# Rounding x_t by a casting DMA from GpSimd instead of by ScalarE, in a gated cross-attention and FFN block

## The reference

```
x   : (4, 512, 512)   ctx : (4, 512, 256)
q   = ctx @ Wq.T + bq ;  k = ctx @ Wk.T + bk             # 128 wide
att = softmax(q @ k.T, axis=-1)                           # (512, 512) a batch
y   = layernorm(x) @ att.T                                # einsum('bln,bmn->blm')
x1  = x + tanh(g_xattn) * y
z   = layernorm(x1) * ln_weight + ln_bias
out = x1 + tanh(g_ffn) * ((z @ sign(W).T) * max|W| * gamma + beta)
```

## Time and profile before

| | us |
|---|---|
| median of 3 runs | 123.74 (123.06 to 123.81) |
| the profiled execution | 123.59 |
| its span (first to last instruction) | 121.8 |
| PE busy | 116.7 (96%) |
| POOL busy | 94.7 (78%) |
| DVE busy | 94.2 (77%) |
| ACT busy | 86.5 (71%) |
| HBM read | 12.59 MB |

### The profile page before, as it was taken

One profiled execution on the slowest core, in us unless ns is written; L12 is line 12 of the kernel. 1 busy time (PEld: TensorE's weight loads), 2 busy tenths in 40 slices (PEclk: granted clock), 3 DMA queues, 4 the chain that ended last, 5 costly groups with the idle time before them and its releaser, 6 DMA issues.

```text
span 121.8 us, 1883 instructions
## 1 busy us (share of the span) xinstructions
PE 116.7 (96%) x565; PEld 94.7 (78%) x565; DVE 94.2 (77%) x186; ACT 86.5 (71%) x184; POOL 94.7 (78%) x108
## 2 busy tenths in 40 slices
PE   7799999999999999999999999999999999999980
PEld 6477887888887877878889888888888888888870
DVE  0159499999888996769966993799849948988991
ACT  3365999999997988476998795659987972245200
POOL 2046995869077998999995999994748999999970
PEclk9999999999999999999999999999999999999999
DMA  3999499833454400027871402457000012220045
GB/s 104 243 378 384 154 405 351 330 112 132 95 192 147 141 31 5 3 86 252 264 258 16 156 5 86 158 181 240 24 3 0 3 63 115 86 86 0 0 154 190
DMA packets 10394, 17.15 MB, mean 141 GB/s; under 512 B 1809, under 2 KB 2321, under 8 KB 10385
## 3 DMA queue, kind: packets, MB, share of 16 engines
q1 hardware_dynamic: 9808, 16.78, 39.9%
q10 hardware_dynamic: 576, 0.26, 0.8%
HBM read 12.59 MB, written 4.19 MB: 138 GB/s over the span
## 4 chain that ended last, share of the span: by engine, by line
PE 92%; DMA 4%; DVE 2%; issue 0%; SPq 0%
PE ps_y L420 37%; PE ps_ffn L433 23%; PE ps_score L355 7%; PE ps_turn L387 6%; DMA ctx_sb<-in_ctx_t_dram 4%; PE ps_score L387 3%; PE ps_y L387 3%; PE ps_ffn L325 2%; PE ps_turn L325 2%; PE ps_y L378 2%; PE ps_turn L355 1%; PE ps_score L364 1%; PE ps_ffn L334 1%; PE ps_y L497 1%; PE ps_ffn L449 1%; PE ps_y L343 1%
## 5 line engine op out<-in xcount | busy, mean ns | idle before, releaser
L915 POOL TENSOR_TENSOR xt_lo<-xt_raw,xt_hi 128x512 fp32r<-128x512 f32 x16 | 21.1, 1319 | 3.9 <-ACT xt_hi L561 2.9
L420 PE MATMUL ps_y<-pt_hi,xt_hi 128*128 128x512 f32 x64 | 18.1, 404 | 0.2 <-issue 0.2
L420 PE MATMUL ps_y<-pt_hi,xt_lo 128*128 128x512 f32 x64 | 17.5, 395 | 0.0
L420 PE MATMUL ps_y<-pt_lo,xt_hi 128*128 128x512 f32 x64 | 17.5, 395 | 0.0
L433 PE MATMUL ps_ffn<-w_sign,zt_hi 128*128 128x512 f32 x60 | 17.2, 408 | 0.0
L433 PE MATMUL ps_ffn<-w_sign,zt_lo 128*128 128x512 f32 x60 | 16.5, 396 | 0.0
L549 ACT ACTIVATE prob<-ps_score,neg_max 128x512 f32<-128x512 f32 x14 | 9.5, 681 | 9.7 <-DVE neg_max L698 9.6
L420 PEld LDWEIGHTS ps_y<-pt_hi,xt_lo 128*128 128x128 f32 x64 | 12.0, 188 | 2.9
L420 PEld LDWEIGHTS ps_y<-pt_lo,xt_hi 128*128 128x128 f32 x64 | 12.0, 188 | 2.9
L420 PEld LDWEIGHTS ps_y<-pt_hi,xt_hi 128*128 128x128 f32 x64 | 11.5, 188 | 2.6 <-issue 0.4
L433 PEld LDWEIGHTS ps_ffn<-w_sign,zt_lo 128*128 128x128 f32 x60 | 11.3, 188 | 2.8
(11 more groups left out here) (184 smaller groups left out, 270.2 us busy)
## 6 DMA issues: line engine op xcount, KB each, us to landing
xt_raw<-in_x_t_dram SPq DMA_DIRECT2D x16, 256.0 KB, 2.9
ctx_sb<-in_ctx_t_dram SPq DMA_DIRECT2D x8, 256.0 KB, 5.2
x_sb<-in_x_dram SPq DMA_DIRECT2D x8, 256.0 KB, 4.4
ctx_sb<-in_x_dram SPq DMA_DIRECT2D x8, 256.0 KB, 5.6
out_dram<-x SPq DMA_DIRECT2D x8, 256.0 KB, 2.0
out_dram<-ctx_sb SPq DMA_DIRECT2D x7, 256.0 KB, 2.1
w_raw<-in_weight_t_dram SPq DMA_DIRECT2D x4, 256.0 KB, 7.0
ln_w<-in_ln_weight_dram SPq DMA_DIRECT2D x1, 256.0 KB, 6.3
```

The source lines that it names most:

```text
L420: mm = pe.matmul(ps_y[t % 2][:, :], lhs[:, t, k, :], rhs[:, k, :], start=(k == 0 and i == 0), stop=(k == KN - 1 and i == 2))
L915: nc.gpsimd.tensor_tensor(xt_lo[:, t, :, :], xt_raw[:, t, :, :], xt_hi[:, t, :, :].bitcast(f32), ALU.subtract).then_inc(xt_lo_done, 1)
```

## The change

In batches 1 to 3, `xt_hi` is no longer written by ACT from `xt_raw`. POOL issues a DMA that reads `x_t` again from HBM and converts float32 to f32r on its way into `xt_hi`. The raw copy is still loaded by SP, and POOL still subtracts. The four DMAs of a `back(b)` stand at four places of POOL's list, and each waits for the same `y_ready` count as the activation did. `attend` and POOL's subtraction wait for a semaphore of the DMA's own.

```
         def attend(b, t):
...
-                pe.wait_ge(xt_hi_done, T * b + t + 1)
+                pe.wait_ge(*((xt_cast[t], 16 * b) if b else (xt_hi_done, t + 1)))
...
         # ScalarE
             def split_xt(b, t):
-                act.wait_ge(xt_in[t], 16 * (b + 1))
-                act.wait_ge(y_ready, T * (b - 1) + t + 1)
-                nc.scalar.activation(xt_hi[:, t, :, :], xt_raw[:, t, :, :], ACT.Copy)\
-                         .then_inc(xt_hi_done, 1)
+                pass
...
         # GpSimd
+            def cast_xt(b, t):
+                pool.wait_ge(y_ready, T * (b - 1) + t + 1)
+                nc.gpsimd.dma_start(xt_hi[:, t, :, :], x_t[b, t, :, :, :]).then_inc(xt_cast[t], 16)
+
             def split_xt(b, t):
-                pool.wait_ge(xt_hi_done, T * b + t + 1)
+                if b > 0:
+                    pool.wait_ge(xt_cast[t], 16 * b)
+                    pool.wait_ge(xt_in[t], 16 * (b + 1))
+                else:
+                    pool.wait_ge(xt_hi_done, T * b + t + 1)
...
             def back(b):
+                cast_xt(b + 1, 0)
                 add_shift(b, 0)
+                cast_xt(b + 1, 1)
                 add_shift(b, 1)
                 if b > 0:
                     power2(b, 0)
...
                 add_shift(b, 2)
                 power2(b, 1)
                 split_xt(b + 1, 1)
+                cast_xt(b + 1, 2)
                 add_ffn(b, 0)
+                cast_xt(b + 1, 3)
                 add_shift(b, 3)
                 add_ffn(b, 1)
                 split_xt(b + 1, 2)
```

More of the change, by code:

```diff
@@ L134, in flamingo_block_kernel @@
         xt_in = [sem(f"xt_in{t}") for t in range(T)]
+        xt_cast = [sem(f"xt_cast{t}") for t in range(T)]
         out_stored = [[sem(f"out_stored{i}_{t}") for t in range(T)] for i in range(2)]
```

## The result

The changed kernel takes 143.26 us (median, 142.59 to 145.07), the kernel before 123.72: a ratio of 1.158 (95% interval 1.154 to 1.163), 15.8% slower. One of its four executions, 145.07 us, had a lower granted clock than the others (0.93 against 0.94 to 0.95); the median of the other three is 142.83. 129.2 was predicted, with a range from 125.2 to 134.0. The sign was right, and 14 us are unaccounted for.

A forecast was written before the change was run, and what follows sets the result against it. PE, busy 96% of the span, was taken as the bound. PE's delay of 5.4 us plus 0.1 us for the last stores made 5.5 us, giving 129.1 from the profiled 123.59; 129.2 us was predicted, range 125.2 to 134.0.

The forecast's parts named there:

- the term for ACT: Twelve activations, 7.4 us, leave ACT; PE never waits for ACT, so worth 0.0, at most 0.2 us.
- The price c: Time that one DMA issue holds POOL: taken as 1.0 us, with 0, 0.44 and 1.3 kept as range.
- Rival 1: The issue on POOL is as cheap as SP's, 0.44 us: 1.7 us of waiting, 125.4 us; chance 0.20.
- The prediction's second estimate: From the Trainium skill's page, 0.4 us on top of SP's 0.44: an issue of 0.84 us, 127.3 us in all.
- Rival 2: The issue runs beside POOL's arithmetic, at most a few hundredths of a us: no change, 123.7 us; chance 0.10.
- Step 1: In back(0), four issues ahead of the third subtraction with 0.06 us slack: PE waits 3.9 us.
- Steps 2 and 3: POOL's gaps close in back(1), no new wait, and in back(2), where PE's total delay becomes 5.4 us.
- the end: POOL's last addition comes 5.8 us later, at 123.2; its store costs 0.1 us beyond PE's 5.4.
- Landing: The first DMA of back(0) lands at 44.1 us, 0.7 us before POOL's subtraction; other transfers have more operations between.
- What it adds: Twelve DMA issues in POOL's list, four per back; the bytes cost nothing by themselves, the y_ready waits hold nothing up.
- the signs of being wrong: Profile signs: gap at 56 us not four issues or before the first pass, POOL's gaps staying, PE waiting for zw or scores.

The follow-up runs named there:

- e13: Kernel before without the twelve roundings of batches 1 to 3, by ACT or DMA; xt_hi keeps batch 0's values: 123.62 us, ratio 0.998.
- e8: Changed kernel with the third and fourth DMA of each back moved up, ahead of scale_x: 126.25 us, ratio 1.019.
- e1: Changed kernel with POOL's own rounding of xt_raw in place of each of the twelve DMAs: 128.38 us, ratio 1.039.
- e10: Changed kernel with two DMAs of two tiles (512 KB) per back in place of four of one tile: 127.08 us, ratio 1.028.
- e6: Kernel before plus twelve POOL copies on all 128 partitions at the places of the DMAs: 127.80 us, ratio 1.031.
- e5: Kernel before plus twelve POOL copies on 32 partitions at the places of the DMAs: 142.17 us, ratio 1.144.
- e4: Changed kernel with tile 0's centring in batches 1 to 3 reading PSUM in place of one SBUF operand: 131.71 us, ratio 1.064.
- e2: Changed kernel with one more POOL wait per back, behind the fourth DMA, for its own preceding addition: 127.63 us, ratio 1.033.
- e9: Changed kernel with ACT rounding tiles 2 and 3 again, DMAs kept for tiles 0 and 1: 125.26 us, ratio 1.014.
- e12: Kernel before plus twelve POOL copies on 32 partitions, each followed by a POOL wait for it to end: 129.47 us, ratio 1.049.
- e7: Kernel before plus twelve POOL DMAs of 8 KB, 64 bytes to each of 128 partitions: 142.19 us, ratio 1.148.
- e3: Kernel before plus twelve POOL DMAs of the same size without conversion, into w_raw's memory: 142.41 us, ratio 1.151.

## Why the prediction was wrong

The kernel before had this view of all its centrings (ns min/median/max):

```profile
L739 DVE SCALAR_TENSOR_TENSOR zw<-x,neg_mean,ln_w x8: 732/1031/1786, 26.6 to 93.4; 128x512 f32<-128x512 f32 x8
L739 DVE SCALAR_TENSOR_TENSOR zw<-ctx_sb,neg_mean,ln_w x8: 732/1495/1895, 52.3 to 111.4; 128x512 f32<-128x512 f32 x8
```

- **What bounds the kernel, and the term for ACT**: right. 0.0 to 0.2 us was said, e13 measured 0.2 us (0.2%) with an interval that ends at no change.
- **The price c**: 1.0 taken, 0.58 measured; it was mis-sized by 0.42. Rival 1's row, SP's issue at 0.44, was nearer than POOL's power at 1.02. By the prediction's own formula, 4c - 0.06, the measured c gives 2.3 us and 126.0, so this term misses by 3 us in the other direction. The prediction's second estimate, 0.84, was too high as well. Rival 2, an issue beside POOL's arithmetic, is out: each issue shows on POOL for 0.57 us or more, and the third subtraction came 2.3 us later (58.21 in place of 55.90).
- **Step 1 (four issues, no slack)**: the mechanism is right where it is alone: e8 grew by 2.3 us of span, e1 waits 2.5 us for the third `xt_lo` with c = 0.61. In the changed kernel the third subtraction ended at 58.21, inside the hole, where PE stood still for `zw` already; the 0.4 us that PE waited for `xt_lo` are those for the second one. So the sign of this kernel's change came out as forecast, but its size has another cause.
- **Steps 2 and 3, the end**: at c = 0.58 the sum has POOL absorbed in `back(1)` and `back(2)`. In the changed kernel it even idled 10.8 us for ACT's squares, late in turn for DVE.
- **Landing**: right, 2.9 us, no slower by the conversion; POOL waited for it only in e10.
- **What failed** is the step "What it adds". It names what stands behind a late DMA "on POOL", subtractions, `scale_x` and `power2`, and takes an issue for a duration in POOL's list, whatever it is made of. It never asks who shares with POOL. With it fails the sentence of step 1 that what stands behind on DVE can be no later than 2c: the centring took 8.76 us, and so ended some 8 us later than at its usual length. DVE's centring was in none of the rivals; a wait of PE for `zw` was only among the signs of being wrong, without a price. The rows were there: the centring took 0.73 to 1.90 us in the kernel before, with the same shape each time, and POOL's additions 1.29 or 1.74. Such a spread beside another engine is a hint of something shared, and the change alters when it is free. The starvation and its clock are 19 us of the 19.2; the wrong c hid 3 us of the miss.
- **The price of a hole in PE** was taken as its length. It was more wherever the clock fell: holes of 7.5, 3.5 and 2.1 us cost another 5.6 us, and e1's 2.5 us another 1.7 in `attend(1, 2)`. In e6's profiled execution a hole of 2.6 us cost no clock. But of e6's four executions two had a mean clock of 1.00 (127.19 and 127.36 us) and two of 0.98 and 0.99 (128.47 and 128.23): the same list of instructions takes about 1 us more or less with the clock.

## What to carry to other kernels

An operation that is put into an engine's list is not only a duration. Before moving a DMA issue, or work on part of the partitions, onto GpSimd, look whether VectorE has operations with two SBUF operands beside GpSimd's long runs, and whether their durations spread in the profile. If so, put such an instruction where GpSimd comes to a stop anyway, or let it wait for one of its own results behind it: one such wait per `back`, three in all, took 15.6 us off here. And when a wait is for an engine whose operation is ten times its usual length, ask what kept that operation out, not what it computes.

## What the runs showed of the hardware

- A DVE operation with two SBUF operands (0.73 us alone) took up to 8.76 us beside POOL operations on tiles that followed each other after a DMA issue, and up to 8.43 us after a copy on 32 partitions (e5). In the changed kernel it ended 0.55 or 0.56 us after POOL's run of such operations ended, in e4 0.83. With one operand in PSUM it took 0.75 us in the same run (e4).
- After copies on all 128 partitions (e6), or where POOL came to a stop behind the DMA or the small copy (e2, e8, e9, e12), no centring took over 2.7 us. Where DVE got in between two operations of POOL in the kernel before, each paid about 0.45 us (1.18 and 1.74 in place of 0.73 and 1.29).
- A DMA issued by POOL held it for 0.56 to 0.58 us in the median for 128 rows of 64 bytes (e7) or of 2 KB (e3, the changed kernel), and for 0.79 us for two pieces of 2 KB per row (e10). The first of an execution took 0.77 to 0.78 us, in e10 0.95. Float32 to f32r on the way did not lengthen the landing: 2.9 us, against 3.0 for the plain DMAs of e3.
- The granted clock fell to its lower level during or after stands of PE of 7.5, 3.5, 2.1 and, in e1 and e12, 2.5 and 2.7 us, and stayed at the full level through a stand of 2.6 us in e6's profiled execution. What decides between the last ones is open.
